# Graph attention: every second unit's ramp made on GpSimd, ramps kept in SBUF, probabilities copied two units at a time

## What is computed

```python
def gat_layer(x, adj, W, a_self, a_neigh, b):
    feat = jnp.einsum('nf,hfo->hno', x, W)
    attn_self = jnp.einsum('hno,ho->hn', feat, a_self)
    attn_neigh = jnp.einsum('hno,ho->hn', feat, a_neigh)
    e = jax.nn.leaky_relu(attn_self[:, :, None] + attn_neigh[:, None, :], 0.2)
    e = e + -1e10 * (1.0 - adj)[None, :, :]
    alpha = jax.nn.softmax(e, axis=-1)
    out = jnp.einsum('hnm,hmo->hno', alpha, feat) + b[:, None, :]
    return jax.nn.elu(jnp.transpose(out, (1, 0, 2)).reshape(out.shape[1], -1))
# per graph: x = x + gat_layer(gat_layer(ctx, adj, W0, ...), adj, W1, ...), adj = layernorm(x)
```

## Time and profile before

| | us |
|---|---|
| median of 3 runs | 2224.22 |
| lowest, highest | 2222.45, 2226.09 |
| span of the profiled execution | 2219.4 |
| DVE, ACT, POOL, PE busy over the span | 1457.5, 1049.0, 881.8, 1828.5 |

### The profile page before, as it was taken

How to read it: one execution, slowest core, us unless ns; L and a number is a source line. 1 busy time by engine, 2 the same in 40 slices (tenths; PEclk the granted TensorE clock), 3 DMA queues, 4 the chain that set the end, 5 groups by cost and what they waited for, 6 DMA issues and landing times. The chain is left out here.

```text
span 2219.4 us, 33593 instructions
## 1 busy us (share of the span) xinstructions
PE 1828.5 (82%) x8271; PEld 893.2 (40%) x8272; DVE 1457.5 (66%) x3126; ACT 1049.0 (47%) x1893; POOL 881.8 (40%) x949
## 2 busy tenths in 40 slices
PE   4689777997439999999963498898899429999997
PEld 2344343444425555555532122222222414444453
DVE  5888887778565655555536477777775675555554
ACT  5587777776413332232315166666667422222222
POOL 5476577666014545555534011111111013444442
PEclk8699998999759999999985599999999759999999
DMA  5111221111637889887647811111111627898984
GB/s 143 53 39 51 75 64 43 39 53 48 216 85 164 180 202 239 189 213 164 111 63 223 139 49 52 46 48 53 53 53 31 231 79 181 226 227 231 229 230 73
DMA packets 202081, 271.15 MB, mean 122 GB/s; under 512 B 83485, under 2 KB 121853, under 8 KB 200957
## 3 DMA queue, kind: packets, MB, share of 16 engines
q1 hardware_dynamic: 156315, 166.52, 24.6%
q0 software_dynamic: 38544, 97.02, 21.9%
q10 hardware_dynamic: 7121, 6.44, 1.5%
HBM read 200.25 MB, written 69.17 MB: 121 GB/s over the span
## 5 line engine op out<-in xcount | busy, mean ns | idle before, releaser
L1890 DVE TENSOR_REDUCE a_negmax<-a_m 128x1 f32<-128x512 f32 x512 | 328.0, 686 | 110.6 <-PE a_m L1747 109.0
L291 POOL TENSOR_TENSOR g_near<-g_mask,g_tb 128x512 f32<-128x512 f32 x256 | 322.6, 1282 | 100.0 <-DVE g_emin L545 99.0
L1839 ACT ACTIVATE a_prob<-a_s 128x1024 f32<-128x1024 f32 x256 | 260.6, 1021 | 143.0 <-PE a_s L1758 134.6
L1282 PE MATMUL f_gu_bank<-f_wgu,f_xT 128*128 x768 | 269.0, 493 | 6.7 <-issue 3.5
L1747 PE MATMUL a_m<-a_kT,a_qT 112*128 (+1 forms) x512 | 198.6, 399 | 72.2 <-DVE a_negmax L1890 38.9
L374 PE MATMUL g_pt<-g_ident,g_p 128*128 128x128 f32 x1024 | 173.2, 298 | 89.8 <-DVE g_pT L554 84.5
L1248 POOL DMA_INDIRECT out<-f_y,f_ids x96 | 151.0, 1573 | 223.3 <-DMA out<-f_y,f_ids 174.2
L1282 PE MATMUL s_gu_bank<-s_wgu,s_xT 128*128 128x512 f32 x512 | 232.2, 596 | 2.3 <-ACT s_xT L1334 1.6
L475 ACT ACTIVATE g_p<-g_e,g_emin 128x512 f32<-128x512 f32 x256 | 183.5, 717 | 97.1 <-DVE g_emin L545 96.4
L374 PEld LDWEIGHTS g_pt<-g_ident,g_p 128*128 128x128 f32 x1024 | 121.9, 150 | 220.1 <-DVE g_pT L554 146.9
L554 DVE COPY g_pT<-g_pt 128x512 f32<-128x512 f32 x256 | 175.3, 685 | 44.9 <-PE g_pt L374 43.5
(11 more groups left out here) (294 smaller groups left out, 2800.7 us busy)
## 6 DMA issues: line engine op xcount, KB each, us to landing
s_wgu<-in_L_ffn_w_gate_up SPq DMA_DIRECT2D x32, 1024.0 KB, 7.5
f_wgu<-in_L_ffn_gate_up_proj SPq DMA_DIRECT2D x32, 768.0 KB, 5.8
s_wd<-in_L_ffn_w_down SPq DMA_DIRECT2D x32, 512.0 KB, 4.1
a_qT<-q_parts SPq DMA_DIRECT2D x217, 64.0 KB, 2.2
g_tb<-neighbours SPq DMA_DIRECT2D x8, 1536.0 KB, 7.6
f_wd<-in_L_ffn_down_proj SPq DMA_DIRECT2D x32, 384.0 KB, 5.7
q_parts<-p_part SPq DMA_DIRECT2D x48, 128.0 KB, 2.3
g_tb<-neighbours SPq DMA_DIRECT2D x8, 512.0 KB, 4.2
```

What stands on the lines that cost most here:

```text
L291: pool.tensor_tensor(near[:, n % LAG, :], mask[slot][:, local % NT, :], t_all[k % SLOTS][:, local // NT, :], ALU.add).then_inc(near_ready, 1)
L1282: last = nc.tensor.matmul(gu_bank[k % TR][:, 0:F], xT[k % TR][:, c, :], wgu[:, bass.ds(place, 1), c, :].rearrange("p a f -> p (a f)"), sta ...
L1839: nc.scalar.activation(prob[n % QR][:, :, :], s_bank[n % RING][:, :, :], ACT.Exp).then_inc(p_ready, 1)
L1890: V.tensor_reduce(negmax[k % RING][:, st, head:head + 1], m_bank[n % RING][:, :], X_AXIS, ALU.max, negate=True).then_inc(m_read, 1)
```

## The change

ACT makes the ramps of even units only, as before but into a ring of four SBUF tiles (`ramp`). The odd units' ramps are made by POOL: max(4t', -4s') with one tensor_scalar, which is relu(4t' + 4s') less 4s', again a row constant that drops out of the softmax. The PSUM banks `h_bank` are gone, and `masked` reads both of its inputs from SBUF. POOL's `near` is made for two units in one instruction of 128x1024, into a ring of 8. The two `pt_bank` buffers hold two units each, and the copy moves two units (128x1024) in one instruction; of the four copies of a pair of heads DVE makes three and ACT the fourth. DVE writes one more small tile per phase (`s_low`, -4s'). Four register loads in the expert stage get bounds.

```diff
-    H_BANKS, PT_BANKS = 2, 2
+    NEARS, RAMPS, PT_PAIRS = 8, 4, 2
+    COPIES = PAIR // 2
+    def ramp_by_act(n):
+        return n % 2 == 0
+    def copied_by_act(u):
+        return u % COPIES == COPIES - 1
...
-        near = sb("g_near", [P, LAG, N])
+        near = sb("g_near", [P, NEARS, N])
+        ramp = sb("g_h", [P, RAMPS, N])
-        h_bank = [stack.enter_context(nc.psum_tensor(f"g_h{i}", [P, N], FP32)) for i in range(H_BANKS)]
-        pt_bank = [stack.enter_context(nc.psum_tensor(f"g_pt{i}", [P, NT, P], FP32)) for i in range(PT_BANKS)]
+        pt_bank = [stack.enter_context(nc.psum_tensor(f"g_pt{i}", [P, 2, NT, P], FP32)) for i in range(PT_PAIRS)]
...
             def _(pool):
                     if layer == 0 and local < NT:
-                        pool.wait_ge(mask_ready, batch * NT + local + 1)
-                    if n >= LAG:
-                        pool.wait_ge(e_ready, n - LAG + 1)
-                    pool.tensor_tensor(near[:, n % LAG, :], mask[slot][:, local % NT, :], t_all[k % SLOTS][:, local // NT, :], ALU.add).then_inc(near_ready, 1)
+                        pool.wait_ge(mask_ready, batch * NT + local + 2)
+                    if n >= NEARS:
+                        pool.wait_ge(e_ready, n + 2 - NEARS)
+                    h, t = divmod(local, NT)
+                    pool.tensor_tensor(near[:, n % NEARS:n % NEARS + 2, :], mask[slot][:, t:t + 2, :],
+                                       bass.AP(t_all[k % SLOTS], h * N, [[H * N, P], [0, 2], [1, N]]), ALU.add).then_inc(near_ready, 1)
+                def ramp_over(n):
...
+                    if local == 1:
+                        pool.wait_ge(s_ready, 2 * (k + 1))
+                    if n >= RAMPS:
+                        pool.wait_ge(e_ready, n - RAMPS + 1)
+                    pool.tensor_scalar(ramp[:, n % RAMPS, :], t_all[k % SLOTS][:, h, :], 4.0, s_low[k % SLOTS][:, t, h:h + 1],
+                                       ALU.mult, ALU.max).then_inc(high_pool, 1)
                 for n in range(ALL_UNITS + 5 * PAIR):
-                    if n < ALL_UNITS:
+                    if n < ALL_UNITS and n % 2 == 0:
                         add_neighbours(n)
+                    if n < ALL_UNITS and not ramp_by_act(n):
+                        ramp_over(n)
...
             def _(pe):
                 def transposes(n):
-                    if n >= PT_BANKS:
-                        pe.wait_ge(pt_ready, n - PT_BANKS + 1)
+                    u = n // 2
+                    if n % 2 == 0 and u >= PT_PAIRS:
+                        wait_copies(u - PT_PAIRS + 1)
...
             def _(act):
+                def copy_probT(u):
+                    act.wait_ge(pt_ps, 2 * u + 2)
...
+                    nc.scalar.activation(probT[:, u // COPIES % RING, hh, :, t * P:(t + 2) * P].rearrange("p c (a n) -> p a c n", a=2),
+                                         pt_bank[u % PT_PAIRS][:, :, :, :], ACT.Copy).then_inc(pt_act, 1)
-                    if n + H_BANKS < ALL_UNITS:
-                        relu(n + H_BANKS)
+                    if n + 2 < ALL_UNITS and ramp_by_act(n):
+                        relu(n + 2)
+                    u = (n - COPY_LAG) // 2
+                    if 0 <= u < ALL_UNITS // 2 and n % 2 and copied_by_act(u):
+                        copy_probT(u)
...
             def _(dve):
-                    V.tensor_tensor_reduce(out=eneg[:, n % LAG, :], in0=near[:, n % LAG, :], in1=h_bank[n % H_BANKS][:, :],
+                    V.tensor_tensor_reduce(out=eneg[:, n % LAG, :], in0=near[:, n % NEARS, :], in1=ramp[:, n % RAMPS, :],
...
-                    V.tensor_copy(probT[:, n // PAIR % RING, hh, :, t * P:(t + 1) * P], pt_bank[n % PT_BANKS][:, :, :]).then_inc(pt_ready, 1)
+                    V.tensor_copy(probT[:, u // COPIES % RING, hh, :, t * P:(t + 2) * P].rearrange("p c (a n) -> p a c n", a=2),
+                                  pt_bank[u % PT_PAIRS][:, :, :, :]).then_inc(pt_dve, 1)
...
-                    e = pe.value_load(table[0:1, bass.ds(j, 1)])
-                    place = pe.value_load(table[0:1, bass.ds(j + P, 1)])
+                    e = pe.value_load(table[0:1, bass.ds(j, 1)], min_val=0, max_val=NE - 1)
+                    place = pe.value_load(table[0:1, bass.ds(j + P, 1)], min_val=0, max_val=RE - 1)
```

More of the change, by code:

```diff
@@ L141, in graph_attention @@
         t_all = [sb(f"g_tb{i}", [P, H, N]) for i in range(SLOTS)]
-        near = sb("g_near", [P, LAG, N])
+        s_low = [sb(f"g_s8n{i}", [P, NT, H]) for i in range(SLOTS)]
+        near = sb("g_near", [P, NEARS, N])
+        ramp = sb("g_h", [P, RAMPS, N])
         eneg = sb("g_e", [P, LAG, N])
@@ L367, in prepare, with wait_copies @@
                             last.then_inc(feat_ps, 1)
+                def wait_copies(u):
+                    by_dve, by_act = copies_of(u)
+                    if by_dve:
+                        pe.wait_ge(pt_dve, by_dve)
+                    if by_act:
+                        pe.wait_ge(pt_act, by_act)
                 def transposes(n):
-                    if n >= PT_BANKS:
-                        pe.wait_ge(pt_ready, n - PT_BANKS + 1)
+                    u = n // 2
+                    if n % 2 == 0 and u >= PT_PAIRS:
+                        wait_copies(u - PT_PAIRS + 1)
                     pe.wait_ge(p_ready, n + 1)
                     for c in range(NT):
-                        last = nc.tensor.transpose(pt_bank[n % PT_BANKS][:, c, :], prob[:, n % PROBS, c * P:(c + 1) * P], ident[:, :])
+                        last = nc.tensor.transpose(pt_bank[u % PT_PAIRS][:, n % 2, c, :], prob[:, n % PROBS, c * P:(c + 1) * P], ident[:, :])
                     last.then_inc(pt_ps, 1)
@@ L456, in relu @@
                             act.wait_ge(t_in[part], 16 * (k + 1))
[L457 to L461, removed]
+                    if n >= RAMPS:
+                        act.wait_ge(e_ready, n - RAMPS + 1)
+                    nc.scalar.activation(ramp[:, n % RAMPS, :], t_all[k % SLOTS][:, h, :], ACT.Relu, scale=4.0,
+                                         bias=s_high[k % SLOTS][:, t, h:h + 1]).then_inc(high_act, 1)
+                def copy_probT(u):
+                    act.wait_ge(pt_ps, 2 * u + 2)
+                    if u >= RING * COPIES:
+                        act.wait_ge(pv_done, u // COPIES - RING + 1)
+                    hh, t = divmod(2 * u % PAIR, NT)
+                    nc.scalar.activation(probT[:, u // COPIES % RING, hh, :, t * P:(t + 2) * P].rearrange("p c (a n) -> p a c n", a=2),
+                                         pt_bank[u % PT_PAIRS][:, :, :, :], ACT.Copy).then_inc(pt_act, 1)
                 for n in range(PREP_FIRST, PREP_FEAT + 10):
@@ L467, in _ @@
                     prepare(0, n)
-                for n in range(H_BANKS):
-                    relu(n)
+                relu(0)
                 for n in range(ALL_UNITS + 2 * PAIR):
@@ L538, in prepare, with copy_probT @@
                         V.tensor_scalar(s_high[k % SLOTS][:, :, :].rearrange("p t h -> p (t h)"), prep_bank[0][:, 0:NT * H], 4.0, None, ALU.mult).then_inc(s_ready, 1)
+                        V.tensor_scalar(s_low[k % SLOTS][:, :, :].rearrange("p t h -> p (t h)"), prep_bank[0][:, 0:NT * H], -4.0, None, ALU.mult).then_inc(s_ready, 1)
                 def masked(n):
[L541 to L542 removed]
+                    if ramp_by_act(n):
+                        dve.wait_ge(high_act, n // 2 + 1)
+                    else:
+                        dve.wait_ge(high_pool, n // 2 + 1)
+                    dve.wait_ge(near_ready, n // 2 + 1)
                     if n >= LAG:
                         dve.wait_ge(p_ready, n - LAG + 1)
[L545 removed]
+                    V.tensor_tensor_reduce(out=eneg[:, n % LAG, :], in0=near[:, n % NEARS, :], in1=ramp[:, n % RAMPS, :],
                                            scale=-1.0, scalar=3.0e38, op0=ALU.add, op1=ALU.min,
                                            accum_out=emin[:, n % LAG:n % LAG + 1]).then_inc(e_ready, 1)
[L549 to L553, removed]
[L554 removed]
+                def copy_probT(u):
+                    dve.wait_ge(pt_ps, 2 * u + 2)
+                    if u >= RING * COPIES:
+                        dve.wait_ge(pv_done, u // COPIES - RING + 1)
+                    hh, t = divmod(2 * u % PAIR, NT)
+                    V.tensor_copy(probT[:, u // COPIES % RING, hh, :, t * P:(t + 2) * P].rearrange("p c (a n) -> p a c n", a=2),
+                                  pt_bank[u % PT_PAIRS][:, :, :, :]).then_inc(pt_dve, 1)
                 def finish(pr, step):
@@ L601, in _ @@
                         masked(n)
-                    if COPY_LAG <= n < ALL_UNITS + COPY_LAG:
-                        copy_probT(n - COPY_LAG)
+                    u = (n - COPY_LAG) // 2
+                    if 0 <= u < ALL_UNITS // 2 and n % 2 and not copied_by_act(u):
+                        copy_probT(u)
                     for pr in pairs_at(n):
@@ L1204, in _ @@
                     else:
```

(4 more changed lines are left out.)

19 lines of the change are left out of this document (13 added, 6 removed).

## The result

The changed kernel takes 2479.75 us (median of 4 runs, 2477.73 to 2480.34) against 2223.34 (4 runs): a ratio of 1.1155, 95% interval 1.1137 to 1.1173. The forecast was 2257 with a range to 2305: the direction holds, the size is off by 223 us.

The account below looks back on a forecast made before the run. No engine was full, DVE nearest; after the change POOL's chain at 3.83 us per two units was to set the attention stage: 467 + 47 + 11 + 12 + 4 = 541 against 507.6, +33 on 2224.2, so 2257 us, range 2215 to 2305.

Parts of the forecast that it names:

- the price of POOL's ramp: Graph attention stage: POOL's 128x512 ramp priced at 0.58 us, bounds 0.56 and 1.28.
- rival 2: Attention stage: turns cost more, or the ramp takes up to 1.28; +103 us, 2327, half of this 2305; chance 13%.
- The turns: DVE's `masked`, now with two SBUF inputs, and POOL's instructions alternate at the SBUF ports; each turn holds POOL 0.44 us.
- rival 1: Attention stage: the custom instruction of `masked` takes no turns, so the kernel gets faster, 2163 us; chance 12%.
- my 3.83: Attention stage: us for two units on POOL, 2.95 for addition and ramp plus 0.88 for two holds.
- my 541: Forecast attention stage in us, first to last `masked`: 467 + 47 + 11 + 12 + 4, against 507.6.
- The mask stretches: Attention stage: 6 pairs of units with mask tiles, DVE and POOL passing a token; 7.8 us a pair, 47 in all.
- The sign I named for the turns: Profile after: `masked` of 0.69 to over 2.5 us, ending some 0.55 behind ends of POOL's instructions.
- DVE's and ACT's savings at nothing: Attention stage: DVE's 46 us and ACT's 33 us less work lie off the path and count for nothing.
- PE's waits gone: Attention stage: DVE's 43.5 us of waits for PE should go, to under 10 us.
- The register loads at 0, at most 10 lost: Expert stage: bounds move register work on PE's sequencer; at most 3.5 us gained or 10 lost, taken as 0.
- the weighing stretch: Attention stage, L504's two-SBUF-input DVE instructions: read as DVE getting its turn between back-to-back POOL additions; costed 4 + 8 us.

Follow-up runs that it names:

- near_pairs: Kernel before with the change's register-load bounds, plus POOL's additions two units at a time in a ring of 8: 2239.34 us, ratio 1.0094.
- spare_ramps: Kernel before with bounds and paired additions; POOL also makes odd units' ramps that nobody reads, ACT makes all ramps into PSUM: 2359.55 us, ratio 1.0614.
- ramp_add: Changed kernel, POOL's ramp adding the per-partition score instead of taking the maximum with it: 2345.05 us, one run.
- mask_later_max: Kernel before, mask tiles five steps later; PE's expert loads unbounded, its waits on the larger of value and 0; SP's and POOL's loads bounded: 2200.48 us, ratio 0.9895.
- ramp_constants: Changed kernel, POOL's ramp taking the constant 0.0 in place of the per-partition score, maximum kept: 2416.47 us, one run.
- ramp_max_alone: Changed kernel, POOL's ramp being only the maximum with the per-partition score, without the factor of 4: 2394.8 us, one run.
- act_ramps: Changed kernel with ACT making all ramps again, still into SBUF; paired additions and copies stay: 2319.24 us, ratio 1.0443.
- sbuf_ramps_only: Kernel before with the bounds, ACT writing its ramps into SBUF tiles instead of PSUM banks: 2293.52 us, ratio 1.031.

## Why the prediction was wrong

| stage, first to last `masked` | us | step |
|---|---|---|
| before | 507.6 | |
| additions in pairs (near_pairs) | 505.6 | -2.0 |
| and POOL's ramps, unread (spare_ramps) | 624.2 | +118.6 |
| all of the change, with the turns (and the paired copies) | 745.0 | +120.8 |

The table's last step is found in full on POOL: against spare_ramps its additions take 345.5 us instead of 302.3 and its ramps 312.5 instead of 256.3, it waits 32.7 us for DVE's mask tiles instead of 15.3, and its ramps wait 6.6 instead of 2.8: 121 us together. So the turns in POOL's instructions cost 99 of the 120.8, and POOL's longer waits, most of them for mask tiles, the rest. The paired copies need not come into it.

- **The step that failed is the price of POOL's ramp.** I took 0.58 us from L269, "the same form but for a per-partition scalar", and 1.28, the two-input price, as upper bound. It is 1.99. The per-partition scalar, which I had doubted, costs 0.07; the second operation, maximum instead of multiplication, which I had not, costs 1.30. The bound was no bound: it came from an instruction with more inputs, while the cost sits in the operation. Put into the sum, even this bound would have given 122 x 0.70 = 85 us more, 2342, beyond the range that I stated; and the "half" of rival 2, written as 2305, is 2224 + 103 / 2 = 2276. With an addition in its place (ramp_add) the kernel takes 2345, so the maximum is worth 135 us.
- **The turns.** That they are taken was right, and rival 1 is out. I took 0.44 us a turn, 0.55 less an overlap of 0.11 that stands in no row. In the profile after it is 2.86 - 2.37 = 0.49 in the addition and 2.50 - 1.99 = 0.51 in the ramp. So of the 1.70 us between my 3.83 and the 5.53 the turns are 0.12, gaps that I had not counted 0.17, and the ramp 1.41.
- **The path with a cheap ramp was wrong too**, and the dear ramp hides it. ramp_add takes 2345, less 19 for the bounds 2326, where I forecast 2257. Its two POOL instructions average 2.47 + 1.07 = 3.54 us, turns included, which is less than my 3.83. But POOL stands 65.0 us for `masked` there (6.6 in the changed kernel), and `masked` takes 1.27 us on the mean. Each engine holds the other up; a sum of POOL's instructions alone, which is what I made, leaves that out.
- **The two together.** In the changed kernel POOL's chain does set the time, as forecast: 2.37 + 1.99 + 0.49 + 0.51 and some 0.17 of gaps are the 5.53 us seen, and 122 x (5.53 - 3.83) = 207 us is nearly the whole miss in the stage (745 against my 541, 204).
- **The mask stretches** were forecast at 47 us and take 57, six times the 9.4 us of a pair, in the same round trip; a ramp of 1.99 instead of 0.58 stands in every second unit of it:

```profile
99.46 0.62 POOL L284 TENSOR_SCALAR g_mask<-g_mask 128x512 f32<-128x512 f32 x1 [1.38 <-DVE g_mask L577]
100.17 1.99 POOL L318 TENSOR_SCALAR g_h<-g_tb,g_s8n 128x512 f32<-128x512 f32 x1
104.57 0.62 POOL L284 TENSOR_SCALAR g_mask<-g_mask 128x512 f32<-128x512 f32 x1 [2.41 <-DVE g_mask L577]
```

- **The sign I named for the turns**, `masked` of 0.69 to over 2.5 us, is there but rare: its mean is 0.78 (200.5 us over 256). DVE mostly waits ahead of the instruction, for the odd unit's ramp or for the addition, and then starts within 0.05 us of POOL's next instruction; it takes its 0.69 us, and POOL's instruction is the longer one. POOL's lengthened instructions are where the turns show.
- **DVE's and ACT's savings at nothing, and PE's waits gone**: right. DVE's copies of 1024 take 1.22 (forecast 1.21), ACT's 1.00, and DVE's wait for PE is 0.7 us. (The 46 us that I had DVE save are 256 x 0.60 - 96 x 1.14 = 44; the sum did not use them.) POOL is the only engine near full.
- **The register loads at 0, at most 10 lost**: wrong, 19 to 23. I read the idle time of PE before the product (3.5 us) as room for gains and named a loss without a row. In mask_later_max both loads stand without bounds and the stretch is back at 484.1 us, with arithmetic on the value in the waits. With one bound of two it stays at 509.7. The counts say why: the two kernels with 192 long pieces of register work on PE take 484.1 and 485.2 us, and all the others, with 384, take 503.4 to 509.7. The bound of `e` adds 192 checks; the bound of `place` only moves the ones that were there.

## What to carry to other kernels

Price an instruction by a row with the same operation on the same engine; where no row has that operation, an upper bound by "more inputs" is none. Before an operand moves from PSUM to SBUF, ask which DVE instruction gets its second SBUF input by it, and what POOL runs beside it: each can hold the other up, and a producer that runs ahead makes it worse. A bound on a loaded register can add a check to the queue of the engine that loads it, or only move one that stands further down: count the register work before and after. A sum over one engine's instructions is a forecast only where the other engine's slots come free in time for it.

## What the runs showed of the hardware that I had not expected

A maximum on GpSimd (128x512, one input, fp32) takes 1.55 us alone and 1.92 to 1.99 behind a multiplication; addition and multiplication in one take 0.62 to 0.69. The Trainium skill ("GPSIMD Engine Reference", section "Engine selection") calls one-input work on this engine roughly line-rate, in its row on adding, multiplying and taking a maximum. With DVE's one-input copy of as many columns (0.68 us) as the measure, the rows agree for the addition and not for the maximum.

DVE doesn't always wait until POOL's instruction ends. In ramp_constants POOL's ramp runs from 310.99 to 312.91:

```profile
310.99 1.92 POOL L318 TENSOR_SCALAR g_h<-g_tb 128x512 f32<-128x512 f32 x1
...
311.03 1.11 DVE L598 CUSTOM_DVE_ANT_0 g_e<-g_near,g_h 128x512 f32<-128x512 f32 x1 [0.81 <-issue]
```

and `masked`, started at 311.03, is done at 312.14, 0.42 late, and POOL's instruction is as long as bare; 105 of the 128 ramps of this run have a `masked` of 1.11 us inside them. In ramp_max_alone, too, some `masked` of 0.81 to 1.08 us lie wholly inside a ramp of 1.56. So POOL stops holding DVE up long before this instruction ends, which would fit a ramp that has read its input early and computes on; that reason is argued, not shown. It is also why ramp_constants gained 63 us over the changed kernel: its ramp is 0.07 shorter and mostly takes no turn of 0.5. Why the ramp with the per-partition score does take it is not shown. The Trainium skill ("SBUF — State Buffer", section "Who interferes with whom") has an exclusive lock on the shared ports, and says, in its item on DVE's two-port modes, that whoever issues first has them for the whole instruction. The additions agree: in ramp_add 92 of the 93 instances of `masked` that last over 0.8 us end 0.54 to 0.57 behind the end of an addition. This ramp does not.

Nor does DVE always get its turn when POOL's instruction ends, as the prediction had read from the weighing stretch. The instances of 8.09 us in act_ramps, and four of 3.94 to 4.85 us in sbuf_ramps_only, run over several additions and finish 0.55 us behind the end of the last. Each of the six starts within 1.2 us of a DMA issue of POOL; why they are passed over is not shown.
